# Mixture of experts in a long one-core kernel: each float32 product written as three float32r products of high and low parts

## What is computed

```
E = 8; K = 2; CAP_RATIO = 1.05
B, S, D, H = (2, 512, 256, 1024)
W1 = ... (E, D, H);  b1 = ... (E, H);  W2 = ... (E, H, D);  b2 = ... (E, D)
```

## Time and profile before

| | us |
|---|---|
| median of three runs | 6387.84 |
| lowest and highest | 6382.72, 6395.87 |
| the profiled execution: time | 6382.99 |
| the profiled execution: span from first to last instruction | 6381.2 |
| of it: from the first hidden matmul of `experts` to its last `y` | 1014.7 |

### The profile page before, as it was taken

The page is one execution under the profiler, slowest core; times in us unless marked ns, Lnnn a source line. Parts: engine busy times, 40 slices in busy tenths (PEclk is TensorE's granted clock), DMA queues, the critical chain, the costliest instruction groups (busy, mean ns, idle before and its releaser), DMA issues. The chain is left out here.

```text
span 6381.2 us, 88977 instructions
## 1 busy us (share of the span) xinstructions
PE 5192.6 (81%) x27631; PEld 2742.2 (43%) x27632; DVE 3185.0 (50%) x6296; ACT 2505.4 (39%) x3173; POOL 1020.5 (16%) x786
## 2 busy tenths in 40 slices
PE   6767777678954999999999999999976059999970
PEld 3434444354422444444444444444335036666650
DVE  4544444331133788888788878888744100000013
ACT  1222333211211477777677767777641012111210
POOL 3430000141123100000000000000014520000016
PEclk8887888889977899999999999999977579999995
DMA  6443333471046433333333333333326321111115
GB/s 215 118 115 109 105 105 106 135 230 56 24 123 182 75 65 64 64 63 64 59 64 64 64 65 65 65 65 55 49 77 206 118 88 54 62 50 53 50 55 182
DMA packets 383841, 578.95 MB, mean 91 GB/s; under 512 B 85288, under 2 KB 279271, under 8 KB 381312
## 3 DMA queue, kind: packets, MB, share of 16 engines
q1 hardware_dynamic: 368736, 524.13, 34.1%
q0 software_dynamic: 14768, 50.51, 2.2%
HBM read 297.62 MB, written 197.24 MB: 78 GB/s over the span
## 5 line engine op out<-in xcount | busy, mean ns | idle before, releaser
L1153 DVE TENSOR_REDUCE full_peak<-full_item 128x1 f32<-128x512 f32 (+2 forms) x3392 | 2036.9, 655 | 466.6 <-PE full_item L1220 461.2
L1123 ACT ACTIVATE full_prob<-full_score 128x1024 f32<-128x1024 f32 (+1 forms) x1792 | 1650.8, 961 | 645.2 <-PE full_score L1231 637.0
L1220 PE MATMUL full_item<-full_kst,full_qst 49*128 49x512 f32 (+1 forms) x4096 | 1204.8, 407 | 43.2 <-DVE full_peak L1153 23.8
L1231 PE MATMUL full_score<-full_qst,full_kst 51*128 51x512 f32 (+1 forms) x3328 | 1110.3, 448 | 17.4 <-ACT full_prob L1123 12.1
L1245 PE MATMUL full_value<-full_prob,full_vaug 128*17 128x512 f32 x6656 | 887.0, 605 | 0.8 <-ACT full_raw L1110 0.7
L1231 PEld LDWEIGHTS full_score<-full_qst,full_kst 51*128 51x128 f32 (+1 forms) x3328 | 480.1, 183 | 931.5 <-ACT full_prob L1123 600.7
L1220 PEld LDWEIGHTS full_item<-full_kst,full_qst 49*128 49x128 f32 x4096 | 630.9, 189 | 188.2 <-DVE full_peak L1153 129.5
L2042 ACT ACTIVATE moe_hT<-moe_hbank,moe_b 128x512 f32<-128x512 f32 (+1 forms) x320 | 199.4, 623 | 806.2 <-PE moe_hbank L2097 801.7
L2109 PE MATMUL moe_ybank<-moe_w,moe_hT 128*128 128x256 f32 x2176 | 488.1, 385 | 5.2 <-ACT moe_hT L2042 5.2
L2097 PE MATMUL moe_hbank<-moe_xT,moe_w 128*128 128x512 f32 (+1 forms) x1280 | 477.4, 531 | 6.7 <-DMA moe_b<-in_b 6.7
L2109 PEld LDWEIGHTS moe_ybank<-moe_w,moe_hT 128*128 128x128 f32 x2176 | 416.5, 193 | 68.3 <-issue 6.0
(11 more groups left out here) (207 smaller groups left out, 5411.9 us busy)
## 6 DMA issues: line engine op xcount, KB each, us to landing
full_kst<-full_high SPq DMA_DIRECT2D x256, 200.1 KB
full_ctxT<-in_ctxT SPq DMA_DIRECT2D x16, 1601.0 KB
full_kst<-full_low SPq DMA_DIRECT2D x128, 200.1 KB
full_qst<-scratch_q SPq DMA_DIRECT2D x384, 64.0 KB
scratch_xbuf<-ctxp_zero POOLq DMA_DIRECT2D x17, 1024.0 KB
scratch_attn<-win_raw SPq DMA_DIRECT2D x64, 256.0 KB, 2.4
scratch_q<-open_parts SPq DMA_DIRECT2D x128, 128.0 KB, 2.3
scratch_attn<-full_raw SPq DMA_DIRECT2D x64, 256.0 KB, 2.1
```

The costliest lines, as they stand in the source:

```text
L1123: nc.scalar.activation(prob[h][(s.par * PAIRS + t) % 2][0:rows, 0:banks, :], score[u % 2][0:rows, 0:banks, :], ACT.Exp, scale=SCALE).then_ ...
L1153: nc.vector.tensor_reduce(peak[s.par][:, hq:hq + len(qts), c], src, AX, ALU.max).then_inc(item_read, 1)
L1220: ins = nc.tensor.matmul(ps[:, at:at + z - a], qst[s.slot][rows, h // 2, qt * P:(qt + 1) * P].bitcast(F32R), kst[s.slot][rows, h // 2, a:z ...
L1231: ins = nc.tensor.matmul(score[u % 2][0:z - a, kt % 2, :], kst[s.slot][rows, h // 2, a:z].bitcast(F32R), qst[s.slot][rows, h // 2, :].bitc ...
```

## The change

A float32 value is split in two: the high part is the value with its low 12 bits cleared (an AND with 0xFFFFF000), the low part is the value less the high part. Both are stored as float32r, a form that TensorE takes in one record per matmul. A product a·b becomes high·high + high·low + low·high; low·low is left out.

- hidden: each matmul becomes three float32r matmuls into the same bank, w1_high x x_high, w1_high x x_low, w1_low x x_high, all of 512 columns.
- rows: h_high stationary and the 512 columns of `w2_both` (high and low beside each other) moving, then h_low stationary and the 256 high columns moving. A bank now holds one tile; its two halves are added by VectorE.
- VectorE: for each k an AND of `h` to `h_cut` and a cast to `h_high`; for each turned half an AND out of PSUM, a cast to `x_high` and a subtraction to `x_low`; for the weights, in 8 pieces of 128x512 per expert, an AND and a cast; and two additions of 256 columns for each tile instead of one of 512 for two. The cast waits for the AND by a semaphore.
- GpSimd: the subtractions `h_low` and `w_low`, each 128x512.
- ScalarE writes `h` into a ring of four; Gelu k waits until GpSimd has read k - 4.
- `h_high` and `h_low` have one buffer each; the raw `w1` and `w2` have one buffer, the split ones two. The pieces of the next expert are split in chunks 1 to 4, two in each, on VectorE between the turned rows and the additions of `y`. Those of the first expert are split before anything else.
- TensorE waits for all eight pieces at the start of an expert, and for `h_high` and `h_low` of each k in the first tile of rows.

```diff
-        w1 = [s.sb(f"w1{i}", [P, KC, HID]) for i in range(2)]
-        w2 = [s.sb(f"w2{i}", [P, HC, D]) for i in range(2)]
+        w1 = s.sb("w1", [P, KC, HID])
+        w2 = s.sb("w2", [P, HC, D])
...
+        h = [s.sb(f"h{i}", [P, SQ]) for i in range(RING)]
+        h_cut = [s.sb(f"h_cut{i}", [P, SQ]) for i in range(RING)]
+        h_high = s.sb("h_high", [P, HC, SQ], F32R)
+        h_low = s.sb("h_low", [P, HC, SQ], F32R)
...
+        @block.gpsimd
+        def _(pool):
+            def low_weights(n, par, j):
+                raw, part, _, (low, low_part) = piece(j)
+                pool.wait_ge(w_cut_done, PIECES * n + j + 1)
+                nc.gpsimd.tensor_tensor(low[par][low_part], raw[part], cut_of(j), ALU.subtract).then_inc(w_low_done, 1)
...
+                    for k in range(HC):
+                        pool.wait_ge(h_cut_done, (n * NC + c) * HC + k + 1)
+                        nc.gpsimd.tensor_tensor(h_low[:, k, 0:cols], h[k % RING][:, 0:cols], h_cut[k % RING][:, 0:cols],
+                                                ALU.subtract).then_inc(h_low_done, 1)
+                    if not last:
+                        for j in PIECES_IN.get(c, ()):
+                            low_weights(n + 1, 1 - par, j)
...
+                        if not (isinstance(n, int) and n == 0 and c == 0 and k < RING):
+                            act.wait_ge(h_low_done, (n * NC + c) * HC + k + 1 - RING)
+                        nc.scalar.activation(h[k % RING][:, 0:cols], hbank[k % 4][:, 0:cols], ACT.Gelu,
...
+            def high_weights(n, par, j):
+                raw, part, (high, high_part), _ = piece(j)
+                if j == 0:
+                    dve.wait_ge(w_in[par], 32 * (n - par) + 64)
+                if not (isinstance(n, int) and n == 0 and j < 2):
+                    dve.wait_ge(w_low_done, PIECES * n + j - 1)
+                nc.vector.tensor_scalar(cut_of(j).bitcast(U32), raw[part].bitcast(U32), HIGH_BITS, None,
+                                        ALU.bitwise_and).then_inc(w_cut_done, 1)
+                dve.wait_ge(w_cut_done, PIECES * n + j + 1)
+                nc.vector.tensor_copy(high[par][high_part], cut_of(j)).then_inc(w_high_done, 1)
...
                 for kc in range(KC):
                     dve.wait_ge(t_full, (n * NC + c) * 2 + kc + 1)
-                    nc.vector.tensor_copy(xT[parity(par, c)][:, kc, 0:cols], tbank[kc][:, 0:cols]).then_inc(t_read, 1)
-
+                    nc.vector.tensor_scalar(x_cut[kc][:, 0:cols].bitcast(U32), tbank[kc][:, 0:cols].bitcast(U32), HIGH_BITS, None,
+                                            ALU.bitwise_and).then_inc(x_cut_done, 1)
+                for kc in range(KC):
+                    dve.wait_ge(x_cut_done, (n * NC + c) * 2 + kc + 1)
+                    nc.vector.tensor_copy(x_high[pg][:, kc, 0:cols], x_cut[kc][:, 0:cols])
+                    nc.vector.tensor_tensor(x_low[pg][:, kc, 0:cols], tbank[kc][:, 0:cols], x_cut[kc][:, 0:cols],
+                                            ALU.subtract).then_inc(t_read, 1)
+
+            def high_hidden(n, c, k):
+                cols = (CHUNKS[c][1] - CHUNKS[c][0]) * P
+                dve.wait_ge(h_read, (n * NC + c) * HC + k + 5)
+                nc.vector.tensor_scalar(h_cut[k % RING][:, 0:cols].bitcast(U32), h[k % RING][:, 0:cols].bitcast(U32), HIGH_BITS,
+                                        None, ALU.bitwise_and).then_inc(h_cut_done, 1)
+                dve.wait_ge(h_cut_done, (n * NC + c) * HC + k + 1)
+                nc.vector.tensor_copy(h_high[:, k, 0:cols], h_cut[k % RING][:, 0:cols]).then_inc(h_high_done, 1)
...
                 for c, (a, z) in enumerate(CHUNKS):
+                    for k in range(HC):
+                        high_hidden(n, c, k)
                     if not (last and c == NC - 1):
                         read_turned(*following(n, par, c))
...
+                    if not last:
+                        for j in PIECES_IN.get(c, ()):
+                            high_weights(n + 1, 1 - par, j)
+                    at_least(dve, y_out[parity(par, c)], before(n, par, c))
+                    for i in range(z - a):
+                        read_rows(n, par, c, i)
...
+                for kc in range(KC):
+                    high, low = (t[par][:, kc, k * P:(k + 1) * P] for t in (w1_high, w1_low))
+                    nc.tensor.matmul(out, high, x_high[pg][:, kc, 0:cols], start=(kc == 0), stop=False)
+                    nc.tensor.matmul(out, high, x_low[pg][:, kc, 0:cols], start=False, stop=False)
+                    ins = nc.tensor.matmul(out, low, x_high[pg][:, kc, 0:cols], start=False, stop=(kc == KC - 1))
...
+                pe.wait_ge(y_read, NY * n + CHUNKS[c][0] + i + 2 * NY - 1)
+                for hc in range(HC):
+                    if i == 0:
+                        pe.wait_ge(h_high_done, (n * NC + c) * HC + hc + 1)
+                        pe.wait_ge(h_low_done, (n * NC + c) * HC + hc + 1)
...
+                pe.wait_ge(w_high_done, PIECES * n + PIECES)
+                pe.wait_ge(w_low_done, PIECES * n + PIECES)
```

111 lines of the change are left out of this document (68 added, 43 removed).

## The result

The changed kernel takes 6419.3 us (median, 6416.6 to 6420.6) against 6388.5 (6382.7 to 6395.9) for the one before: a ratio of 1.0044, with a 95% interval of 1.0032 to 1.0057. It is slower by 31 us, more than the 13 us that can be told from no change. The forecast was 6400 with a range of 6340 to 6520. The profiled executions are 6381.2 us long before and 6417.6 after, 36.4 apart.

The account below looks back on a forecast made before the run. TensorE bound the kernel before; its gain would be taken back by VectorE and GpSimd taking turns. Seven experts unchanged, start +15, last expert -3, together +12 on 6383.0, 6395, with 4.9 to the median 6400; range 6340 to 6520.

Parts of the forecast that it names:

- The bound and the mechanism: Full chunks: VectorE and GpSimd take turns, and late `y` of tile 0, at 22.9 us, holds back the third tile.
- The price of float32r: TensorE's matmuls in hidden and rows: one pass, 0.214 us for 512 columns, hidden 10.3 us instead of 13.7.
- the case of two passes: Rival for TensorE's matmuls: float32r needs two passes on the full array, chunks of 42 us, 6850; chance 0.03.
- The step of k: AND, cast and subtraction for each k of hidden, on VectorE and GpSimd in turn: 1.83 us, between 1.74 and 1.94.
- In chunks 1 to 3 the loss hides under VectorE's late y: TensorE's lowered clock costs nothing extra in these chunks; 1.5 us was added for chunk 0, 3.7 an expert in all.
- A gap of TensorE before the third tile of rows, ended by VectorE's y: Sign expected in the trace of chunks 1 and 2: TensorE idle there until VectorE delivers `y`; no size given.
- The sum: One expert: 25.6 + 2 x 28.2 + 26.5 + 15.3 + 3.7 = 127.5 us; seven 892.5 against 892.3 before.
- The start: Before the first hidden: 8 weight pieces and the turned rows are split first, +15 us with the earlier landing.
- The last expert: It has no weight pieces to split: 119 us to the last `y` against 122.4, -3.
- Whole records in turn: Rival: VectorE and GpSimd alternate without overlap, 2.15 us for a k, 139 an expert, 6494; chance 0.10.
- the slow casts: Rivals, VectorE's cast at 0.69 us: holding the port, 2.12 a k, 6516, chance 0.12; leaving it free, 6370, chance 0.10.
- No turns at all: Rival: VectorE and GpSimd work side by side, only GpSimd's 1.27 us a k counts, 6231; chance 0.15.

Follow-up runs that it names:

- clock_fill: Changed kernel, with TensorE multiplying by tiles of zeros during its waits in the first tile of rows of full chunks; 6410.8 us.
- y_first: Changed kernel, with VectorE taking the next expert's weight pieces behind the `y` of the second tile of rows instead of ahead of all `y`; 6432.1 us.
- fill_and_y_first: Changed kernel with both edits, TensorE's waits filled with products of zeros and the second tile's `y` ahead of the weight pieces; 6368.4 us.
- narrow_vector: Changed kernel, with VectorE's AND and cast on `h` working on 16 columns instead of 512, so not the same product; 6271.1 us.
- dve_balanced: dve_alone, with weight pieces behind the second tile's `y`, spread three, three and two over chunks 1 to 3, none in the tail; 6220.5 us.
- dve_alone: Changed kernel, with all of GpSimd's subtractions moved to VectorE behind the cast, GpSimd idle in the stage; 6307.7 us.

## Why the prediction was right, and where its sizes were off

**The bound and the mechanism: right.** VectorE's `y` of tile 0 was walked out at 22.9 us after the start of hidden. In chunk 1 of the changed kernel it is 5247.03 - 5224.08 = 22.95. Tile 2 starts 0.6 us later than the forecast's 22.9 + 0.1, at 5247.67 - 5224.08 = 23.6, because tile 1 at half clock ends after `y`: the length of the chunk came out near the forecast by two delays that happen to be nearly equal, of which the forecast charged one.

**The price of float32r: too low.** Six matmuls of hidden should stand 0.214 us apart. They are 0.229 apart, three steps in 0.69 (two records left out):

```profile
5224.77 0.39 PE L2181 MATMUL moe_hbank<-moe_x_high,moe_w_high 128*128 128x512 f32 x1
...
5225.46 0.39 PE L2181 MATMUL moe_hbank<-moe_x_high,moe_w_high 128*128 128x512 f32 x1
```

Hidden is 48 x 0.229 = 11.0 us, not 10.3. In the rows a pair of 512 and 256 columns takes 0.353 us (5239.58 to 5242.05 in clock_fill is seven pairs), not 0.321, and a tile 2.83, not 2.57. One pass it is; the case of two passes fell. These 0.26 us a tile, twice behind the late `y`, are 0.5 of the 0.8 to 0.9 us by which chunks 1 and 2 are longer than the 28.2 of the forecast.

**The step of k: near, in part by luck.** 1.86 to 1.90 us, on the mean 1.89, against 1.83, of 1.74 to 1.94. The cast is 0.427 (0.42 taken). The 1.83 was between two orders, 1.74 with the cast first and 1.94 with the subtraction first. In all 256 steps of full chunks the cast came first, by 0.04 us, and so the order that occurs had been priced 0.15 too low. In the rows shown the subtraction ends 1.14 us behind the cast (5230.31 - 5229.17) where I had 1.07, and the next AND 0.3 behind that where I had 0.21. The subtraction's 1.27 us are recorded as 1.53, with the wait for the cast in them.

**"In chunks 1 to 3 the loss hides under VectorE's late y": right for 1 and 2, wrong for 3.** clock_fill, y_first and fill_and_y_first show the cover for 1 and 2. So does the changed kernel by itself: in chunk 2 of the second and of the seventh expert the clock had not fallen in tile 1, tile 2 waited 1.93 us for `y` instead, and it began 4.9 us after tile 1 as in the others. Chunk 3 turns only the tail, so its `y` comes only 0.6 us after a tile 1 at full clock (the wait in clock_fill), while at the fallen clock tile 1 takes 1.2 to 2.3 us more (4.1 to 5.1 instead of 2.83). Most of the clock's loss shows, as in chunk 0: 28.0 us against 26.5, and 26.8 with the filling. This is the step that failed, with 1.2 to 1.5 us in each expert.

**"A gap of TensorE before the third tile of rows, ended by VectorE's y" as the sign of it: wrong as a sign.** The wait for `y` is 6.7 us in all chunks together, because TensorE was still busy with tile 1, in most chunks at half clock. From this one number the late `y` looks harmless; y_first, tried for 55 us, gained none of them. Only the two edits together show its price.

**The sum.** It was 27.1 (25.6 and 1.5 of clock), 28.2, 28.2, 26.5 and 17.5 (15.3 and 2.2 of clock) for one expert, 127.5. Measured from Gelu to Gelu it is 27.6, 29.0, 29.1, 28.0 and 16.2, together 129.8; from hidden to hidden 130.1. So the four full chunks are 0.5 to 1.5 us longer and the tail is 1.3 shorter, and seven experts are three quarters of the missing 24 us (18.4 instead of 0.2). In the seven tails the turn begins 6.3 to 7.8 us after the first hidden matmul, 6.8 on the mean as in the forecast. It takes 1.1 us in three of them, as below, and 1.6 to 2.0 in four: 0.4 more than at full clock on the mean, where 0.9 had been added. GpSimd's last piece ends at 14.7 on the mean, forecast with the clock for 15.6, and the next expert begins 0.2 behind it instead of 0.6.

```profile
5317.83 1.09 PE L2172 MATMUL moe_tbank<-moe_ident,moe_x 128*128 128x128 f32 x8 [0.86 <-DMA moe_x<-scratch_xbuf]
```

The start was +14.5 for +15. The last expert was -0.5 for -3. With the waits filled (clock_fill) its full chunks take 26.8, 26.7, 26.7 and 26.7 us where the forecast had 25.6 for each: this is the higher price of the step and of float32r, 4.4 us more in all. Without the filling they are 6.2 us longer together, where 7.3 had been added for the clock. The 4.7 us ahead of the stage stand in no step; they are spread. "Slower" had the largest chance of the three, 0.43; the time of 6400 was 19 us too low. That it lies so near owes something to errors of opposite sign: full chunks 3.7 us an expert too short, the tail 1.3 too long.

**The rivals.** Whole records in turn (2.15 a step) and the slow casts (2.12) fall by 1.9 us and by 0.427. Of the rule of the Trainium skill, page "SBUF — State Buffer", section "Who interferes with whom", that a 2-port operation of VectorE and GpSimd block each other completely, the runs bear out the block for AND and cast. The subtraction alone takes 1.293 us and with AND and cast at 0.427 each this would be 2.15 if no part overlapped; the measured step is 1.90, so the completeness that the page states is not borne out to the last 0.25 us. That the two engines only disturb each other over one buffer is ruled out by the code: the AND of k + 1 reads and writes other ring buffers than the subtraction of k, and waits all the same. No turns at all would have been 6231; narrow_vector, in which only the weight pieces still take turns in full, has 6271.

## What to carry over

When work is taken off the engine that sets the time and put on two others, look first whether those two can work side by side: one row in which an operation beside the other engine is recorded at several times its own length is a warning (4.55 us instead of 1.20 before the change, 1.3 to 1.5 instead of 0.43 after it). Here all of it on one engine was faster (1.40 us a step instead of 1.90), and that engine kept a reserve in every chunk. And where two delays end at the same instruction, an edit that removes one shows little; remove both before calling either harmless.

## What the runs showed of the hardware

VectorE's AND of a tile in SBUF is held up by GpSimd's subtraction; its AND out of `tbank` and its additions out of `ybank` (both in PSUM) are not. In the changed kernel 50 of the 64 full-width ANDs of `x` begin while a subtraction runs; they take 0.68 us on the mean, and the other 14 take 0.69. Of the 256 ANDs of `h`, the 222 that begin so take 1.43 us and the others 0.43. The operations from PSUM also run at a slower pace of their own (0.69 us against 0.43 for 512 columns), and VectorE's subtraction with both inputs in SBUF never ran beside GpSimd; so these runs do not show which property decides. At the first expert's start an AND from SBUF takes 1.48 us beside a subtraction, and two ANDs from PSUM, the first of them wholly beside one, take 1.28 together, as they do in dve_balanced where GpSimd has nothing to do:

```profile
5188.01 1.48 DVE L2109 TENSOR_SCALAR moe_w_cut<-moe_w 128x512 uint32<-128x512 uint32 x1
...
5189.57 1.50 POOL L2066 TENSOR_TENSOR moe_w_both<-moe_w,moe_w_cut 128x512 fp32r<-128x512 f32 x1 [0.36 <-DVE moe_w_cut L2109]
5189.87 1.28 DVE L2119 TENSOR_SCALAR moe_x_cut<-moe_tbank 128x512 uint32<-128x512 uint32 x2
```

In chunk 0 of the first expert the granted clock fell to 1.2 GHz in the matmul behind three waits of 1.17, 1.27 and 1.24 us with 0.6 us of work between them, in chunk 1 behind waits of 0.17, 1.27 and 1.28 us. In chunk 0 of the second expert it stayed at 1.00 through tile 1 behind waits of 1.16 and 1.28. It stayed up in all these places where 0.9 us of each wait were filled with products of zeros. float32r with all 128 rows of the array costs 0.229 us for 512 columns. In dve_alone, where GpSimd is idle, VectorE's subtraction with both inputs in SBUF takes 0.684 us for 512 columns, its AND 0.421 and its cast to float32r 0.427.
